# Summing the value products in SBUF instead of a reserved PSUM bank, with one transpose for the maxima and unrolled image loops

## The reference, cut to what matters

```python
h = group_norm(x)                              # 8 groups
q, k, v = h @ qkv_w                            # layer 0: one head of 128
x = x + softmax(q k^T / sqrt(128)) v @ proj_w  # 1024 x 1024 scores per image
t = tokens(x)
sq, sk, rv = ln(t) @ (wq_s, wk_s, wv_r)        # layer 1: 8 heads of 16, 2 value sets
retrieved = softmax(sq sk^T / 4) @ rv          # 8 x 1024 x 1024 scores per image
gate = softmax over the 2 value sets of (rq . retrieved @ wk_ret)
t = t + (sum of gate * retrieved) @ w_out
t = t + ln(t) @ dequant_nf4(qidx, scales)^T @ W^T
```

## Time and profile before

| | |
|---|---|
| median of 3 runs | 4804.96 us (4800.92 to 4805.71) |
| profiled execution | 4802.95 us |
| its span | 4801.1 us |
| TensorE clock granted, mean | 0.986 |
| PE / POOL / DVE / ACT busy | 96% / 88% / 81% / 69% of the span |

### The profile page before, as it was taken

One profiled execution on the slowest core, in us unless ns is written; L12 is line 12 of the kernel. 1 busy time (PEld: TensorE's weight loads), 2 busy tenths in 40 slices (PEclk: granted clock), 3 DMA queues, 4 the chain that ended last, 5 costly groups with the idle time before them and its releaser, 6 DMA issues.

```text
span 4801.1 us, 102107 instructions
## 1 busy us (share of the span) xinstructions
PE 4608.7 (96%) x29838; PEld 2533.9 (53%) x29838; DVE 3906.7 (81%) x8190; ACT 3317.4 (69%) x6657; POOL 4242.2 (88%) x1142
## 2 busy tenths in 40 slices
PE   5899999999999999999999999999999999999985
PEld 4555555555555555555555555555555555555532
DVE  4788888888888888888888888888888888888863
ACT  2567777777777777777767777767777777777654
POOL 1589999999999999999999999999999999999996
PEclk9899999999999999999999999999999999999987
DMA  1011111111111111111111111111111111111010
GB/s 33 23 45 45 50 32 45 32 45 45 49 32 45 32 45 45 49 32 45 32 45 45 49 32 45 32 45 46 49 32 46 31 45 49 45 32 49 24 40 14
DMA packets 92739, 191.77 MB, mean 40 GB/s; under 512 B 16744, under 2 KB 50920, under 8 KB 92400
## 3 DMA queue, kind: packets, MB, share of 16 engines
q1 hardware_dynamic: 92400, 186.45, 13.9%
HBM read 17.53 MB, written 16.78 MB: 7 GB/s over the span
## 4 chain that ended last, share of the span: by engine, by line
PE 85%; DVE 6%; ACT 4%; issue 3%; POOL 1%; SPq 0%; DVEq 0%; ACTq 0%; DMA 0%; POOLq 0%
PE ps_u L804 18%; PE ps_bank L769 13%; PE ps_bank L791 11%; PE ps_bank L755 10%; PE ps_bank L741 4%; PE ps_bank L679 4%; DVE max_part L1067 4%; PE ps_bank L690 3%; PE ps_bank L710 3%; ACT p L962 3%; PE ps_bank L813 3%; PE ps_bank L743 3%; PE ps_bank L744 2%; PE ps_bank L742 2%; DVE max_part L1051 2%
## 5 line engine op out<-in xcount | busy, mean ns | idle before, releaser
L645 POOL TENSOR_TENSOR p_sum<-p_sum,p 128x2048 f32<-128x2048 f32 x768 | 3510.8, 4571 | 363.6 <-ACT p L962 316.6
L1067 DVE TENSOR_REDUCE max_part<-ps_bank 128x1 f32<-128x512 f32 x4096 | 2570.5, 683 | 513.0 <-PE ps_bank L769 500.8
L962 ACT ACTIVATE p<-ps_bank 128x512 f32<-128x512 f32 x4096 | 2153.3, 612 | 564.4 <-PE ps_bank L791 553.4
L804 PE MATMUL ps_u<-p,rv 128*32 128x512 f32 x8192 | 996.8, 604 | 3.2 <-ACT u_sb L968 2.5
L769 PE MATMUL ps_bank<-k_stack,q_stack 63*128 63x512 f32 x4096 | 863.5, 451 | 65.4 <-DVE max_part L1067 17.7
L791 PE MATMUL ps_bank<-q_stack,k_stack 64*128 64x512 f32 x4096 | 839.8, 449 | 35.2 <-ACT p L962 20.2
L791 PEld LDWEIGHTS ps_bank<-q_stack,k_stack 64*128 64x128 f32 x4096 | 372.0, 186 | 518.9 <-ACT p L962 177.0
L645 POOL TENSOR_TENSOR p_sum<-p 128x2048 f32<-128x2048 f32 x128 | 584.1, 4563 | 69.3 <-ACT p L962 69.3
L769 PEld LDWEIGHTS ps_bank<-k_stack,q_stack 63*128 63x128 f32 x4096 | 372.4, 185 | 507.6 <-DVE max_part L1067 199.2
L755 PE MATMUL ps_bank<-v,p 128*128 128x129 f32 x4096 | 498.9, 277 | 2.6 <-ACT p L919 1.6
L755 PEld LDWEIGHTS ps_bank<-v,p 128*128 128x128 f32 x4096 | 471.9, 191 | 38.1 <-DVE t_front L1097 12.5
(11 more groups left out here) (139 smaller groups left out, 4475.8 us busy)
## 6 DMA issues: line engine op xcount, KB each, us to landing
k_stack<-k_hi SPq DMA_DIRECT2D x256, 128.0 KB, 2.6
q_stack<-q_hi SPq DMA_DIRECT2D x256, 128.0 KB, 2.8
x_sb<-in_x SPq DMA_DIRECT2D x32, 512.0 KB, 3.6
k_stack<-k_lo SPq DMA_DIRECT2D x128, 128.0 KB, 2.6
q_stack<-q_lo SPq DMA_DIRECT2D x128, 128.0 KB, 2.8
t_held<-t_front SPq DMA_DIRECT2D x32, 512.0 KB, 2.9
rqk<-tok_next SPq DMA_DIRECT2D x32, 512.0 KB, 3.6
t_core<-t_held SPq DMA_DIRECT2D x32, 512.0 KB, 3.9
```

What stands on the lines that cost most here:

```text
L645: pool.tensor_tensor(p_sum[:, phase % 2, :, :], before, p1[:, step % ring, :, :], ALU.add)\
L804: last = pe.matmul(ps_u[n * QUAD:(n + 1) * QUAD, :], rv[:, key_tile, :], p1[:, step % ring, n, :], start=(key_tile == 0), stop=(key_tile = ...
L962: act.activation(p1[:, step % ring, n, :], bank_of("scores", index // 2, n % 2), ACT.Exp, scale=scale1)\
L1067: dve.tensor_reduce(max_part1[:, phase % 2, i, n, half:half + 1], bank_of("max1", index // 2, side), AXIS.X, ALU.max)\
```

## The change

Per image, unless said otherwise:

1. `ps_u` is gone and `ps_bank` has eight banks. A `values` visit writes to a bank of the rotation, starts and stops its own accumulation there, and is read at once: the first visit of a phase by an ACT copy (`take_u`, 4, replacing 4 `evict_u`), the other three by a DVE add into `u_sb` (`add_u`, 12). `u_sb` has two slots.
2. `max_rows1` is one transpose instead of four (so 4 instead of 16) with an ACT copy of 16 x 128; `max_rows0` is one transpose instead of 8 with one ACT copy of 8 x 128 and a new DMA, `row0`, to the row that `score0` reads.
3. The loop is written out: all passes are straight code, and every wait compares with a constant.
4. The decode of the FFN weight moves from setup to image 0, on DVE behind `max0_last`; its folding product goes into the bank of the last `value0` of image 0. Setup loads are split over the SP and ACT queues with `qkv_w` and `x` first; the setup tiles lie in `p1` instead of `p0`. `prod` has one slot instead of two.
5. All five orders are new. As shapes of the PE array, the PE list read entry by entry is:

```diff
-    for b in range(last + 1 - images, first):
-        turn_of(b)
...
-    with nc.Fori(first + 1, last + 1, engines=[engine.engine], hint_back_edge=True) as b:
...
+    for b in range(last + 1 - images, first + images):
         turn_of(b)
...
                 def values(b, visit, at):
                     phase = 2 * visit // tiles
                     if visit == 0:
+                        pe.wait_ge(ffn_w_ready, 1)
                         pe.wait_ge(rv_ready, 1 * (b + 1))
-                    if 2 * visit % tiles == 0:
-                        wait(pe, u_evicted, phases * b + phase)
+                    part = visit % visits_per_phase
                     pe.wait_ge(p1_ready, weights_per_image * b + 2 * GROUP * (visit + 1))
+                    if part == 0:
+                        out = open_bank(at[0], u_taken, phases, phase + 1)
+                    else:
+                        out = open_bank(at[0], u_added, phases * u_adds, u_adds * phase + part)
...
+                            last = pe.matmul(out[n * QUAD:(n + 1) * QUAD, :], rv[:, step % tiles, :],
+                                             p1[:, step % ring, n, :], start=(step % 2 == 0), stop=(step % 2 == 1))
...
+                def add_u(b, visit):
+                    phase, part = divmod(visit, visits_per_phase)
+                    if part == 1:
+                        dve.wait_ge(u_taken, phases * b + phase + 1)
+                    else:
+                        dve.wait_ge(u_added, u_adds * (phases * b + phase) + part - 1)
+                    dve.wait_ge(values_done, visits * b + visit + 1)
+                    dve.tensor_tensor(u_sb[:, phase % 2, :], u_sb[:, phase % 2, :], bank_of("values", visit), ALU.add)\
+                       .then_inc(u_added, 1)
...
                 def max_rows1(b, phase, at):
-                    for i in range(tiles_per_half):
-                        last = pe.transpose(out[:, i * P:(i + 1) * P], max_cols1[:, GROUP * i:GROUP * i + P], ident[:, :])
-                    last.then_inc(filled["max_rows1"], 1)
+                    pe.transpose(out[:, 0:P], max_cols1[:, 0:P], ident[:, :]).then_inc(filled["max_rows1"], 1)
...
+                def row0(b, index):
+                    sp.wait_ge(max_tile0_ready, 1 * (b + 1))
+                    wait(sp, filled["score0"], halves * tiles * b)
+                    sp.dma_start(max_row0[0:1, :].bitcast(F32), max_tile0[:, :].bitcast(F32)).then_inc(row0_moved, 16)
```

More of the change, by code:

```diff
@@ L32 @@
 NF4_BLOCK = 16
-BANKS = 7
+BANKS = 8
 PE_ORDER = """
[L38 to L62, removed]
@@ new lines @@
+max_rows1.1@0/0 score0.12@1/4 max1.33@0/37 max1.34@0/10 max1.35@0/56 values.3@0/2 max1.36@0/43
+ln2_channels.0@-1/7 scores.16@0/10 score0.13@1/2 ln2_channels.1@-1/5 score0.14@1/1 ffn.0@-1/6 score0.15@1/0
+scores.17@0/47 scores.18@0/32 scores.19@0/51 value0.4@1/0 result.0@-1/4 max1.37@0/67 scores.20@0/32
+scores.21@0/51 values.4@0/0 scores.22@0/46 scores.23@0/37 max1.38@0/25 max1.39@0/10 max1.40@0/46 max1.41@0/23
+value0.5@1/5 value0.6@1/7 value0.7@1/1 scores.24@0/04 scores.25@0/62 max1.42@0/53 values.5@0/7 den.0@0/0
@@ new lines @@
+max0.7@2/43 values.11@0/2 scores.48@0/57 max1.0@1/01 max1.1@1/64 scores.49@0/53 scores.50@0/07 max_rows0.0@2/1
+scores.51@0/53 max1.2@1/60 max1.3@1/47 max1.4@1/25 scores.52@0/31 values.12@0/6 scores.53@0/03 max1.5@1/14
+max1.6@1/72 score0.0@2/6 scores.54@0/50 max1.7@1/13 den.2@0/4 scores.55@0/67 max1.8@1/52 max1.9@1/01
+turn_den.2@0/4 score0.1@2/3 max1.10@1/65 scores.56@0/72 values.13@0/4 scores.57@0/03 max1.11@1/17 max1.12@1/62
+max1.13@1/54 turn_u.2@0/0 score0.2@2/1 score0.3@2/3 score0.4@2/7 score0.5@2/6 max1.14@1/13 max1.15@1/27
@@ L66 @@
+scores.58@0/54 score0.6@2/6 score0.7@2/5 scores.59@0/04 scores.60@0/16 scores.61@0/32 value0.0@2/5 value0.1@2/7
+value0.2@2/0
 """
 ACT_ORDER = """
[L69 to L72, removed]
@@ L118 @@
+add.11@0 ln1_rstd.0@1 add.12@0 add.13@0 norm_rstd.0@2 add.14@0 add.15@0 add.17@0 add.18@0 add.19@0 add.20@0
+add.21@0 add.22@0 add.23@0 add.25@0 add.26@0 add.27@0 add.28@0 add.29@0
 """
 SP_ORDER = """
-load.0@2 rows.1@0 take_rqk.0@0 store.0@-1 rows.2@0 stack.0@1 take.0@0 rows.3@0 hold.0@1 rows.0@1 stack.1@1
+rows.0@0 stack.1@0 rows.1@0 store.0@-2 take_rqk.0@0 take.0@0 hold.0@1 rows.2@0 stack.0@1 rows.3@0 load.0@3
+row0.0@2
 """
@@ L218, in in_order @@
     last = images - 1 - max(ahead for _, _, ahead, _ in order)
-    for b in range(last + 1 - images, first):
-        turn_of(b)
-    before = links.count if links else 0
-    turn_of(first)
-    per_turn = links.count - before if links else 0
-    with nc.Fori(first + 1, last + 1, engines=[engine.engine], hint_back_edge=True) as b:
-        if banks:
-            banks.image = Image(b, banks.image - first - 1, 0)
-        if links:
-            links.looped = (b - first - 1) * per_turn
-        turn_of(b)
-    if banks:
-        banks.image = last + banks.image.ahead
-    if links:
-        links.looped = (last - first - 1) * per_turn
-    for b in range(last + 1, first + images):
+    for b in range(last + 1 - images, first + images):
         turn_of(b)
@@ L756, in value0 @@
                                          start=(key_tile == 0), stop=(key_tile == tiles - 1))
+                    if b == 0 and query_tile == tiles - 1:
+                        pe.wait_ge(codes_decoded, 1)
+                        last = pe.matmul(out[:, 2 * P:3 * P], lora, turned[:, 1, :], start=True, stop=True)
                     last.then_inc(filled["value0"], 1)
```

275 lines of the change are left out of this document (149 added, 126 removed).

## The result

The kernel after takes 4838.8 us (median of 4 runs, 4837.8 to 4842.8), the kernel before 4805.3: a ratio of 1.0072 [1.0058, 1.0085]. It is slower by 0.7%, small but outside the interval, where 4643 was forecast and 4545 to 4750 was the range.

What follows compares the result with a forecast made beforehand. PE was taken as the bound, POOL close behind. -5.3 (PE work) + 0.5 (DVE adds) - 0.3 (loop) = -5.1 us per image over 30 images, -153, and -7 at the ends: 4803 to 4643 us, range 4545 to 4750.

Steps and rivals of the forecast that it cites:

- Fewer transposes: On PE, 19 transposes fewer per image at 0.11 us each: 2.1 us less, bounds 0.5 to 2.1.
- fewer shape changes: On PE, array shape changes per image fall from 105 to 89, at 0.2 us each: 3.2 us less, bounds 0 to 3.2.
- Rival B: PE's saving mostly taken back, as DVE and POOL pace it: period 141 to 144, 4710 to 4803 us; chance 0.18.
- POOL's floor: POOL's untouched adds: no reordering brings the period under 143.9 - 9.85 = 134.05 us.
- rival A: Holes before POOL's adds close: period 134.05 to 136.5, 4500 to 4573 us, though some hole stays; chance 0.13.
- The stretch of 24 entries: New PE list between scores of steps 15 and 16, the longest without scores; leaves POOL a hole of some microseconds.
- The loop: Written-out passes remove PE's issue holes behind the jump: -0.3 us per image, bounds -0.3 to 0, same fetches.
- The clock: TensorE's granted clock read as 1.00, the 2.4 GHz level, in the steady stretch 2000 to 3000.
- DVE's adds: 12 add_u put 8.3 us per image on DVE, mostly covered by idle time: +0.5 us, bounds -1 to +8.3.
- adds exposed in full: A rival: each add delays DVE's bank reads, +8.3 us on PE, net +2.7 per image, 4877 us; chance 0.07.
- Setup: Earlier loads and the decode moved off setup: -8 us once, net -7 with the first image's longer maxima path.
- the marks for "wrong": PE waiting for DVE over 3 us an image, POOL idle still near 10, or issue holes on PE in straight code.

Runs made afterwards that it cites:

- a_loop: The kernel after with its steady images back in a loop instead of written out; 4808.2 us, ratio 1.0017.
- a_fill: The kernel after with three pairs of row-half products per image made twice, just ahead of where the clock falls; 4809.0 us, ratio 1.0014.
- a_loop_fill: The kernel after with the loop restored and three pairs of row-half products made twice per image; 4770.5 us, ratio 0.9934.
- b_unroll: The kernel before with its 28 looped passes written out, order and stages untouched; 4819.2 us, ratio 1.0032.
- b_mr1: The kernel before with one transpose instead of four for max_rows1, all lists unchanged; 4795.3 us, ratio 0.9978.
- b_join: The kernel before with seven PE entries moved so that short runs of row-half pairs join; 5127.1 us, ratio 1.0675.
- a_fastread: The kernel after with score exponentials on 128 of 512 columns and max1 reduces on 64, part of the computation left out; 4690.6 us, ratio 0.9770.
- a_add1: The kernel after with DVE's 12 value-product adds per image cut to one column of 512; 4819.3 us, ratio 1.0031.
- b_mr1_rot2: The kernel before with one max_rows1 transpose, value products in their own bank summed by ACT copies and DVE adds, take_u.2 later on ACT; 4830.1 us, ratio 1.0059.

## Why the prediction was wrong, step by step

Forecast was a period of 138.8, measured 145.9. The difference of 7.1 us per image, split along one path (the clock first, then the loop; by a_loop first, the loop and the stretches that go with it are 1.3 and the doubled pairs 1.3):

| part | us per image | shown by |
|---|---|---|
| half-clock stretches | 1.1 | after 145.87, a_fill 144.77 |
| straight code | 1.5 | a_fill 144.77, a_loop_fill 143.27 (0.7 in b_unroll) |
| waits in place of PE's saved work | 4.5 | a remainder, 143.27 - 138.8; b_mr1 shows its kind |

- **Fewer transposes, fewer shape changes** (-2.1 and -3.2): right as work. PE has 608 = 19 x 32 instructions fewer, and by starts 5.1 us less. No run tests the shape changes by themselves, since b_join lost to its bank numbers.
- **The step that failed is the one that carried this into the period**: "PE's starts follow each other tightly nearly everywhere, so I take 3.2", and then -5.1 summed over 30 images. With less work between its entries PE reaches the same banks sooner and waits. b_mr1 shows it for the transposes, with every list unchanged: 1.8 us less work, 0.5 less period at full clock, 1 us more of listed waits for ACT and DVE. For the rest of the saved work it is inferred: with the loop back and the clock up (a_loop_fill) the period is 143.27, only 0.6 us under before, for 5 us less work. Rival B named this; its period of 141 to 144 holds a_loop_fill's 143.3, not after's.
- **POOL's floor** was read as 134.05 and the hole as "some microseconds" in rival A only, when the sum needed it. The forecast left POOL 4.7 us of idle time in all; the one hole is 7.07 us in a_loop_fill, and 5.8 even with both readers fast (a_fastread). 134.05 + 5.8 = 139.8 is over the forecast of 138.8 before straight code has any price. The stretch of 24 entries had been counted (seven of them `max1`, not six). What it costs wasn't put into the likeliest case.
- **The loop** (-0.3): wrong in sign. The `issue` waits of PE did go, but they weren't the price. POOL's sums start 0.06 us later in straight code (b_unroll), and POOL runs them back to back for most of an image. Fetches were not fewer: q8 and q14 have 253 + 175 packets and 5.58 MB in after, 311 + 28 and 5.33 MB in before. That they cause the delay isn't shown.
- **The clock** was taken as 1.00 because the earlier trace rows has 1.00. Images that gain waits of 0.2 us in a row can lose it, and three of four did.
- **DVE's adds** (+0.5): 0.3 to 0.6 by a_add1, right for their length on DVE. In the old order, adds, copies and waits together cost 1.1 (b_mr1_rot2). DVE is 87% busy, not 93%, since the period is longer. The sentence of the Trainium skill (page "TensorEngine Tiling (Array Packing)", section PSUM Bottleneck) that reading of PSUM may become the bottleneck was closer than my weighing of it: fast readers give back 3.2 us an image to before and 3.7 to after, at full clock. I had weighed it for DVE alone, while the waits that PE's listing names are mostly for ACT. The outcome that the prediction drew from it, adds exposed in full, did not come.
- **Setup** (-7 once): right. Images begin at 15.54 (22.34 in the earlier trace rows), and the first sum starts at 153.50 (161.24 in the earlier trace rows). The decode sits behind `max0_last` at 40.4 and takes 6.2 us, where 14.2 were forecast: its 15 operations take 2.12 us here and 10.57 in the earlier trace rows, where POOL was clearing `k_stack` and `q_stack` beside them (4.07 to 11.02 us). Setup and first image of the kernel after:

```profile
15.54 1.29 DVE L1014 BATCH_NORM_STATS2 stat<-x_sb 128x6 f32<-128x512 f32 x2 [0.32 <-PEq L374]
...
40.38 0.22 DVE L1045 CAST p<-p 128x128 f32<-128x128 int32 x1
40.64 2.12 DVE L1048 TENSOR_SCALAR p<-p 128x128 f32<-128x128 f32 x15
...
46.30 0.29 DVE L1051 TENSOR_TENSOR p<-p,block_scale 128x128 f32<-128x128 f32 x1
...
153.50 4.55 POOL L632 TENSOR_TENSOR p_sum<-p 128x2048 f32<-128x2048 f32 x1 [68.20 <-ACT p L951]
```

- **What would show it**: of the marks for "wrong", POOL's idle near 10 came (214.6 us in 20.6 images, 10.4 each). The other two did not: PE waits for DVE 7.7 us in 20.6 images in the listing, and has no `issue` holes. The waits are mostly for ACT, which no mark named. Two readings were off by little: of the 14.5 us before reduces of `max1`, 14.1 are waits for PE (293.6 / 20.85), and rival B's 144 gives 4799, not 4803.

What stays open: of the last 4.5 us, fast readers give 3.7 at full clock (144.77 to 141.12 among images without a stretch), and POOL's hole would hold the rest (139.8 - 138.8); the two overlap, and no run parts them cleanly. Fast readers help before nearly as much, so they say what both kernels wait for, not which new place in the list costs what.

## What to carry to other kernels

Work taken off the busiest engine of a hand-ordered rotation is not time until the next constraint has been priced in full: compute the other engine's floor with its longest hole, and compare that with the forecast first. Where PE shows waits of 0.2 us in a row, look at the granted clock window by window; a few doubled products can be cheaper than the stretch at half clock. When a list is edited, bank numbers and the readers' lists must move with the entry: one ACT copy in the wrong place cost 98 us here and six moved PE entries 238, more than any part of the change.
